# Attention and mixture of experts in one kernel: routing steps placed inside the attention loop

## What is computed

```python
h = _layernorm(x, axis=-1) * (1 + ca) + sa
x = x + ga * _L0_attn_ref(h, ...)        # 16 heads of 16 channels, softmax over 1024 keys
h = _layernorm(x, axis=-1) * (1 + cb) + sb
x = x + gb * _L0_ffn_ref(h, ...)
...
scores = sigmoid(xf @ gate_weight.T)     # 32 experts in 8 groups
sfc = scores + e_score_correction_bias   # best 4 groups by maximum, then best 6 experts
tw = scores of the 6, divided by their sum, times 2.5
routed = sum over the 6 experts of tw * (silu(g) * u) @ down.T
shared_out = (silu(xf @ shared_gate_w.T) * (xf @ shared_up_w.T)) @ shared_down_w.T
return routed + shared_out
```

## Time and profile before

| | us |
|---|---|
| runs | 1714.81, 1718.88, 1721.71 (median 1718.88) |
| the profiled execution | 1716.23 |
| its span, first to last instruction | 1714.5 |
| VectorE busy in the span | 1267.9 (74%) |
| TensorE busy (products) | 1355.5 (79%) |
| ScalarE busy | 795.5 (46%) |
| GpSimd busy | 432.8 (25%) |
| mean granted TensorE clock | 0.885 of full speed |

### The profile page before, as it was taken

One profiled execution on the slowest core, in us unless ns is written; L12 is line 12 of the kernel. 1 busy time (PEld: TensorE's weight loads), 2 busy tenths in 40 slices (PEclk: granted clock), 3 DMA queues, 4 the chain that ended last, 5 costly groups with the idle time before them and its releaser, 6 DMA issues. The chain is left out here.

```text
span 1714.5 us, 33047 instructions
## 1 busy us (share of the span) xinstructions
PE 1355.5 (79%) x8063; PEld 693.4 (40%) x8064; DVE 1267.9 (74%) x3027; ACT 795.5 (46%) x1195; POOL 432.8 (25%) x454
## 2 busy tenths in 40 slices
PE   7963999999998999999937666671299999999800
PEld 4530222233332333322215444441177777777700
DVE  7865999999997999999225677774056555555579
ACT  4650177777776777777812211220033333333300
POOL 0000000000000000000010677777455555555500
PEclk9985599999999999999977878785599999999955
DMA  7857833232222222200064456435765555555497
GB/s 249 257 190 111 178 86 73 66 79 66 63 66 45 68 69 74 65 15 15 20 154 105 153 169 196 152 111 195 264 177 171 166 168 168 169 173 167 132 377 315
DMA packets 221129, 237.34 MB, mean 138 GB/s; under 512 B 96797, under 2 KB 188317, under 8 KB 220898
## 3 DMA queue, kind: packets, MB, share of 16 engines
q1 hardware_dynamic: 191426, 162.23, 35.8%
q0 software_dynamic: 20096, 62.83, 9.6%
q10 hardware_dynamic: 9504, 11.01, 1.8%
HBM read 130.83 MB, written 105.14 MB: 138 GB/s over the span
## 5 line engine op out<-in xcount | busy, mean ns | idle before, releaser
L568 DVE TENSOR_REDUCE piece_max<-psM 128x1 f32<-128x512 f32 x1024 | 634.5, 681 | 34.5 <-PE psM L641 30.6
L623 ACT ACTIVATE probs<-psE 128x1024 f32<-128x1024 f32 x512 | 498.2, 1021 | 227.9 <-PE psE L651 226.4
L641 PE MATMUL psM<-k_main,q_main 48*128 48x512 bf16 x1024 | 319.3, 403 | 59.5 <-DMA v_cols<-v_values 40.9
L663 PE MATMUL psO<-probs,v_cols 128*32 128x512 f32 x2048 | 274.8, 609 | 0.6 <-ACT probs L623 0.6
L1330 POOL DMA_INDIRECT results<-ex_y,ex_pair x223 | 213.7, 958 | 187.6 <-DVE ex_y L1314 122.8
L651 PE MATMUL psE<-q_main,k_main 49*128 49x512 bf16 x1024 | 246.7, 382 | 5.9 <-issue 3.5
L651 PE MATMUL psE<-q_rest,k_rest 48*128 48x512 bf16 x1024 | 246.1, 381 | 0.0
L1242 PE MATMUL ex_psGU<-gu_w,ex_xT 128*128 x892 | 233.2, 384 | 0.7 <-ACT ex_xT L1274 0.5
L641 PEld LDWEIGHTS psM<-k_main,q_main 48*128 48x128 bf16 x1024 | 74.4, 93 | 384.7 <-DVE piece_max L568 308.9
L707 POOL DMA_INDIRECT lists<-rows,slot x192 | 193.0, 1005 | 58.7 <-issue 58.7
L824 POOL MEMSET ones<- 128x128 bf16 x1 | 0.2, 205 | 754.2 <-POOLq L424 754.2
(11 more groups left out here) (167 smaller groups left out, 1363.5 us busy)
## 6 DMA issues: line engine op xcount, KB each, us to landing
ex_rows<-lists SPq DMA_DIRECT2D x223, 160.0 KB, 2.8
six<-results SPq DMA_DIRECT2D x16, 1536.0 KB, 10.0
qk_parts<-parts SPq DMA_DIRECT2D x32, 384.0 KB, 2.6
xin<-in_x_dram SPq DMA_DIRECT2D x16, 512.0 KB, 5.0
v_values<-vst SPq DMA_DIRECT2D x32, 256.0 KB, 3.5
v_cols<-v_values SPq DMA_DIRECT2D x16, 512.0 KB, 4.5
gu_w<-in_guT_dram SPq DMA_DIRECT2D x8, 1024.0 KB
q_main<-qk_parts SPq DMA_DIRECT2D x96, 64.0 KB, 2.9
```

The lines of the kernel that those rows point to most:

```text
L568: nc.vector.tensor_reduce(piece_max[:, (x * PAIRS + h) * KT + qt, kh:kh + 1], psM[:, n % RING], AX.X, ALU.max).then_inc(piece_read, 1)
L623: nc.scalar.activation(probs[:, s % 2, 2 * pair:2 * pair + 2], psE[:, pair], ACT.Exp, scale=HD ** -0.5).then_inc(exp_ok, 1)
L641: nc.tensor.matmul(psM[:, n % RING], qa[g][rows, h, qt * P:(qt + 1) * P], ka[g][rows, h, kh * 512:(kh + 1) * 512], start=True, stop=True). ...
L663: mm = nc.tensor.matmul(psO[32 * h:32 * h + 32], va[g][:, kt, 32 * h:32 * h + 32], probs[:, s % 2, 2 * pair + x], start=(kt == 0), stop=(k ...
```

## The change

All of routing but the last chunk moves into the attention loop, where `route_phase` had it behind. Chunk c (its heads are groups 2c and 2c+1) is routed in window c, the 32 steps that begin with step 32(c+1). `w` is the step in the window, and `d = 4w + n` the place beside the n-th piece of that step, at which VectorE does one part of `route_part`. TensorE's products for routing (two halves of the projection, two halves of the turn, gate, placement) go into the `psM` slot of the next step's first piece, at w = 9, 10, 20, 21, 22, 28. ScalarE copies the turned tile out and takes the sigmoid. GpSimd adds the bias to `x`, normalises and modulates, and scatters.

The softmax sums are now stored as 16 equal rows per head, loaded spread (`inv`, 1024 per partition), and inverted and multiplied there by VectorE (d = 24, 25); `den`, `invert` and its DMAs are gone. The standard deviation's inverse comes from an integer first guess and three rounds of Newton on VectorE (19 small instructions with mean and variance) in place of ScalarE's square root. The experts are picked by `max` and `match_replace` in place of `max_index` and one-hot tiles. The turned tiles of chunks 0 to 5 are kept in DRAM (`h2T_d`).

Behind attention, without a barrier between, `closing_phase` routes chunk 7 and computes the shared expert of all eight chunks, in the order 6, 0 to 5, 7. SP, no longer ScalarE, writes the pads, and the table goes out behind them. The first row load of the experts waits for `y_read`, the last shared expert. Weights of the experts are loaded over the q and k tiles in attention's last batch. The batches are written out, with no loop.

Helpers and parts (TensorE, ScalarE, VectorE):

```diff
+def slot_of(step):
+
+    return 4 * ((step + 1 + AHEAD) % STEPS) % RING
...
+def project_half(pe, env, c, half, to):
+
+    if half == 0:
+        pe.wait_ge(env.vals_ok, c + 1)
+        pe.wait_ge(env.wo_ok, c // CPB + 1)
+    out = to.rearrange("p (i d) -> p i d", i=TPC // 2)
+    for i in range(TPC // 2):
+        at = (half * TPC // 2 + i) * P
+        for m in range(KC):
+            mm = env.nc.tensor.matmul(out[:, i], env.vals[:, m, at:at + P], env.wo_g[:, m], start=(m == 0),
+                                      stop=(m == KC - 1))
+    mm.then_inc(env.projected, 1)
...
+def turn_half(pe, env, c, k, to):
+
+    if k == 0:
+        pe.wait_ge(env.h2_ok, c + 1)
+    for i in range(TPC):
+        mm = env.nc.tensor.transpose(to[:, i * P:(i + 1) * P], env.rows_of(c)[:, i, k * P:(k + 1) * P], env.ident[:])
+    mm.then_inc(env.turned, 1)
...
+def gate(pe, env, c, to):
+
+    pe.wait_ge(env.h2T_ok, KC * (c + 1))
+    for i in range(TPC):
+        for k in range(KC):
+            mm = env.nc.tensor.matmul(to[:, i * E:(i + 1) * E], env.h2T_of(c)[:, k, i * P:(i + 1) * P], env.gate_w[:, k],
+                                      start=(k == 0), stop=(k == KC - 1))
+    mm.then_inc(env.gated, 1)
...
+def place(pe, env, c, to):
+
+    pe.wait_ge(env.sel_ok, c + 1)
...
+def turned_out(act, env, c, k, of):
+
+    act.wait_ge(env.turned, KC * c + k + 1)
+    if k == 0:
+        wait(act, env.h2T_out, 16 * min(c, LAST - 1))
+    env.nc.scalar.activation(env.h2T_of(c)[:, k], of, ACT.Copy).then_inc(env.h2T_ok, 1)
...
+def scores_of(act, env, c):
+
+    act.wait_ge(env.logits_read, c + 1)
+    wait(act, env.routed, c)
+    env.nc.scalar.activation(env.sc[:].rearrange("p i e -> p (i e)"), env.logits[:], ACT.Sigmoid).then_inc(env.sc_ok, 1)
...
+    if d == 24:
+        dve.wait_ge(env.vals_in, 16 * VALS_LOADS * (c + 1))
+        then(v.reciprocal(env.inv[:].rearrange("p k n -> p (k n)"), env.inv[:].rearrange("p k n -> p (k n)")))
+    elif d == 25:
+        ready()
+        v.tensor_tensor(env.vals[:], env.vals[:], env.inv[:], ALU.mult).then_inc(env.vals_ok, 1)
+    elif d in (40, 44):
+        half = (d - 40) // 4
+        dve.wait_ge(env.projected, 2 * c + half + 1)
+        dve.wait_ge(env.biased, c + 1)
+        pair = slice(half * TPC // 2, (half + 1) * TPC // 2)
+        v.tensor_tensor(env.x2[:, TPC * c + 2 * half:TPC * c + 2 * half + 2], of.rearrange("p (i d) -> p i d", i=2),
+                        env.xin[:, pair], ALU.add).then_inc(env.x2_ok, 1)
+    elif d == 42:
...
+    elif d == 92:
+        dve.wait_ge(env.gated, c + 1)
+        wait(dve, env.sc_ok, c)
+        v.tensor_copy(env.logits[:], of[:, 0:TPC * E]).then_inc(env.logits_read, 1)
+    elif d == 100:
+        dve.wait_ge(env.sc_ok, c + 1)
+        then(v.tensor_tensor(env.sfc[:], env.sc[:], bc(env.ebias[:].unsqueeze(1), TPC, E), ALU.add))
...
+    elif d == 109:
+        ready()
+        then(strike(env.masked, env.keys, env.unmasked))
...
+    elif d == 116:
+        dve.wait_ge(env.placed, c + 1)
+        wait(dve, env.placed_read, c)
+        then(v.tensor_tensor(env.slot[:], of[:, 0:TPC * E].rearrange("p (i e) -> p i e", i=TPC),
+                             bc(env.following[:, c % 2].unsqueeze(1), TPC, E), ALU.add))
+        v.tensor_tensor(env.following[:, (c + 1) % 2], of[:, TPC * E:(TPC + 1) * E], env.following[:, c % 2], ALU.add
+                        ).then_inc(env.placed_read, 1)
...
+def scale_out(dve, env, b):
+
+    v = env.nc.vector
+    wait(dve, env.projected, 2 * CPB * b)
+    wait(dve, env.biased, CPB * b)
+    ga = env.modb[:, b, 0]
+    v.tensor_tensor(env.wo_g[:], env.wo[:], ga.unsqueeze(1).to_broadcast([P, KC, D]), ALU.mult).then_inc(env.wo_ok, 1)
+    v.tensor_tensor(env.bo_g[:], env.bo_bc[:], ga, ALU.mult).then_inc(env.bo_ok, 1)
```

In `attention_phase` (in this order: helpers, SP, GpSimd, VectorE, TensorE):

```diff
+        def chunk_at(step):
+
+            c, w = divmod(step, WINDOW)
+            return c - 1, w
+
+        def pieces_for(step):
+
+            ahead, share = divmod(step + AHEAD, STEPS)
+            return ahead + 1, 4 * share
...
+            def store(group):
+                b, g = divmod(group, NG)
+                sp.wait_ge(o_read, QH * (group + 1))
...
+                    for to, at in ((env.o_d, 2 * HD * j), (env.s_d, 2 * HD * j + HD)):
+                        sp.dma_start(to[b, g * HG + j].rearrange("r d a -> d r a"), o_sb[at:at + HD]
+                                     ).then_inc(o_stored, 16)
...
+            def load_values(c):
+                b, u = divmod(c, CPB)
+                sp.wait_ge(o_stored, 16 * 2 * HG * 2 * (c + 1))
+                wait(sp, env.projected, 2 * c)
+                wait(sp, env.h2_ok, c)
+                for m in range(KC):
+                    for to, of in ((env.vals, env.o_d), (env.inv, env.s_d)):
+                        sp.dma_start(
+                            to[:, m].rearrange("p (h a) -> p h a", h=H // CPB),
+                            of[b, u * H // CPB:(u + 1) * H // CPB].rearrange("h (m r) d a -> m (r d) h a", m=KC)[m]
+                            ).then_inc(env.vals_in, 16)
...
+            for group in range(NGR):
+                b, g = divmod(group, NG)
+                c = group // 2 - 1
+                if g % 2 and 0 <= c < LAST - 1:
+                    store_turned(c)
+                if group + 1 < NGR:
+                    put_max(group + 1)
+                if g % 2 == 0 and c >= 0:
+                    load_x(c + 1)
+                if b < B - 1:
+                    sp.wait_ge(summed, STEPS * (group + 1))
+                    load(b + 1, g)
+                elif g < NG - 1:
+                    sp.wait_ge(summed, STEPS * (group + 1))
+                    load_gate_up(sp, env, GU_PART * g, GU_PART * (g + 1))
+                store(group)
+                if g % 2:
+                    load_values(group // 2)
 
         @block.gpsimd
...
+            def normalise(c):
+                b = c // CPB
+                pool.wait_ge(env.inverted, c + 1)
+                if c:
+                    pool.wait_ge(env.scattered[(c - 1) % CPB], 16 * TPC * TOPK * ((c - 1) // CPB + 1))
+                for i in range(TPC):
+                    ins = g.tensor_scalar(env.xhat[:, i], env.x2[:, TPC * c + i], env.mean[:, i:i + 1],
+                                          env.rstd[:, i:i + 1], ALU.subtract, ALU.mult)
+                chain.link(ins)
+                chain.link(g.tensor_tensor(env.xhat[:], env.xhat[:],
+                                           env.modb[:, b, 2].unsqueeze(1).to_broadcast([P, TPC, D]), ALU.mult))
+                g.tensor_tensor(env.rows[:, :, 0:D], env.xhat[:],
+                                env.modb[:, b, 1].unsqueeze(1).to_broadcast([P, TPC, D]), ALU.add).then_inc(env.h2_ok, 1)
...
+            add_bias(0)
+            for c in range(LAST):
+                normalise(c)
+                add_bias(c + 1)
+                pool.wait_ge(env.routed, c + 1)
+                scatter_chunk(nc, env, c)
...
+            def beside(step, n):
+                c, w = chunk_at(step)
+                if c >= 0:
+                    if w == 0 and n == 0 and c == 0:
+                        dve.wait_ge(env.consts, CONSTS)
+                    route_part(dve, env, steps, c, 4 * w + n, psM[:, slot_of(step - 1)])
+                if w == 18 and n == 0 and c % CPB and c < LAST:
+                    scale_out(dve, env, (c + 1) // CPB)
...
+            dve.wait_ge(const_in, 16 * 6)
+            for step in range(-AHEAD, ALL):
+                group, first = pieces_for(step)
+                for n in range(4):
+                    beside(step, n)
+                    if group < NGR:
+                        piece_maximum(group, first + n)
+                if group < NGR and first + 4 == PIECES:
+                    finish(group)
...
+            def route_products(step):
+
+                c, w = chunk_at(step)
+                if c < 0 or w not in (PROJECT, PROJECT + 1, TURN, TURN + 1, GATE, PLACE):
+                    return
+                to = psM[:, slot_of(step)]
+                group, n = pieces_for(step + 1)
+                pe.wait_ge(piece_read, min(PIECES * group + n - RING + 1 if n else PIECES * group, PIECES * NGR))
+                if w in (PROJECT, PROJECT + 1):
+                    project_half(pe, env, c, w - PROJECT, to)
+                elif w in (TURN, TURN + 1):
+                    turn_half(pe, env, c, w - TURN, to)
+                elif w == GATE:
+                    gate(pe, env, c, to)
+                elif w == PLACE:
+                    place(pe, env, c, to)
+
+            def slot_free(step):
+
+                c, w = chunk_at(step - 1)
+                if c < 0:
+                    return
+                if w in (PROJECT, PROJECT + 1):
+                    pe.wait_ge(env.x2_ok, 2 * c + w - PROJECT + 1)
+                elif w in (TURN, TURN + 1):
+                    pe.wait_ge(env.h2T_ok, KC * c + w - TURN + 1)
+                elif w == GATE:
+                    pe.wait_ge(env.logits_read, c + 1)
```

(93 more changed lines are left out.)

902 lines of the change are left out of this document (407 added, 495 removed).

## The result

The changed kernel takes 1805.67 us (median of 4 runs, 1802.8 to 1809.32) against 1720.3 for the kernel before, measured beside it: ratio 1.0503, 95% interval 1.047 to 1.0535. It is slower by 85 us. 1722 had been forecast, with a range up to 1765, so the time lies outside the range.

What follows compares the result with a forecast made beforehand. VectorE, busy 601 of 621 us, was taken to bound attention, and a chain over the engines routing. A tail shorter by 240.6 us against terms of +245 gave +4, about 1722 us on the median's scale, range 1680 to 1765.

Steps and rivals of the forecast that it cites:

- Start, +13: Attention's start: VectorE waits for the constants before the first pieces of group 1; 13 us more, bounds 7 and 14.
- Unrolling: Attention loop: straight-line code has no jump back and no half clock after it; 10 us saved.
- VectorE's work: Routing instructions added to VectorE in attention, 19.3 us a chunk; 127 us more, bounds 115 and 145.
- The late load, +63: At w=6, values land ten microseconds late behind SP's next-batch loads: six times 10, 3 for chunk 6; bounds 54 and 87.
- rival D: Values land still later because the previous chunk's scatter falls on SP's loads and stores; 6 us more gives 1758; chance 0.15.
- ScalarE's tables, +8: In attention, the sigmoid's table load and reloading Exp's, 2.84 us in a stretch; 8 us more, bounds 0 and 15.
- GpSimd beside VectorE, +5: At w=18, only scale_out can meet GpSimd's normalise or add_bias: 2.3 us, at most four times; 5 us more.
- Clock behind the load +14: After the wait for values and the reciprocal, TensorE restarts at half clock: 2 us a chunk, 14 together; bounds 0 and 35.
- handover +32: Six routing products each take a psM ring slot, causing idles: 5 us a chunk, 2.5 for chunk 6; bounds 10 and 50.
- B: In attention, small VectorE work and ring reads fill the handovers and table loads: 40 us less, 1682; chance 0.15.
- C: At w=6 the values are in time, so the 63 and 14 us fall away: 1645; chance 0.07.
- E: TensorE becomes attention's bound: slot waits keep it at half clock for seven more steps a chunk, +45: 1767; chance 0.13.

Runs made afterwards that it cites:

- The change of order: Changed kernel with SyncE's queue issuing a finished group's stores and the four value loads ahead of the next batch's 25 loads: 1717.76 us, ratio 0.9986.
- the version with the four edits: Changed kernel with stores and values first, constants awaited at first use, sigmoid from the exponential, scaling at w=12: 1668.34 us; again on another chip 1666.89.

## Why the prediction was wrong

**What bounds, and the tail: right.** The line of the earlier trace rows that says VectorE has nothing to spare held: the waits taken off it in the experiments came out as time. The tail was 128 us where 124 was forecast (112 to 140), and the shared experts end it, as the sum had it, though the pads took 11 us longer than the sum allowed.

**Start, +13: right in kind, measured 17 in the profile.** The constants were issued at 203.1 to 205.6 rather than near 201.7, behind the maxima, and the first pieces came at 212.27 rather than 194.87. Worth 12 to 17.

**Unrolling, VectorE's work and the reciprocal: right.** The loss at the loop jump is gone: of the idle before the reductions only the start's 14.9 us are still put down to "issue"; how much unrolling won no run separates. VectorE's busy time from 202 to the end of attention grew from 602.9 to 741.3 us; less 7 for reductions that lay ahead of 202 before and 8 for the lock below, and with the 8 of the old inverses, its routing work is 131 where 127 was forecast. The reciprocal is 6.55 us for 1024 against 6.2 from a 64-element row; 6.1 by its removal.

**The late load, +63: measured 96. This is the step that failed most.** Its mechanism was the right one, and its place too, but its size was wrong three times. In chunks 0 to 5 I took 10 us from the queue's order. The order alone makes 11.3 (the window without scatters, and the five behind it with them held), 8 us more over the six; the scatters of the chunk before, which the forecast kept for rival D as a cause by itself, add 3 in each of chunks 1 to 5, 16 together. And in chunk 6, "one large weight load stands there instead: 3" was a guess by the number of instructions in the queue. With that transfer ahead and the scatters beside it the issue of the stores was held (6.15 us for one), and the wait was 12.2, 9 more; why an issue is held so long is not shown. The change of order shows what the step as a whole was worth, 88 us.

**ScalarE's tables, +8: measured about 34** (some 10 either way). I counted the two loads against ScalarE's slack and took the rest as hidden behind VectorE's other holds. The loads stop TensorE for 2.4 us, and behind that its clock is at 0.50 for some 10 us, in which VectorE waits for pieces again. The forecast looked for half clock only behind the late values.

**GpSimd beside VectorE, +5: measured about 15** (some 10 either way). The lock lies where it was said to lie, three times and not four; what was missed is again what came behind it: with VectorE held 2.7 us longer, ScalarE stood 4.1 and TensorE 3.2 us.

**Clock behind the load +14, handover +32: 54 left for both.** What is left, 328 less 17 (start), 96, 34, 15, VectorE's work of 129 (127 and 0.35 for each of seven longer reciprocals) and plus the 17 saved by unrolling and old inverses, is 54; it carries the uncertainty of the others, the 17 of unrolling and inverses being the forecast's own. Idles of 11 to 13 us a window, beyond the waits for values, are left in the version with the four edits too, so they don't come from the late load. No run separates handover from clock here; that stays open. One reason given for the clock term was misread: the row at 204 to 206 shows half clock with TensorE counted busy for all 2 us, and from 160 to 192 of that trace too it is counted busy all the time at 0.50, with some 18 products in 10 us. So idling is not what that row shows; with the reciprocal in four, too, the clock fell while TensorE had little work but no long stop.

So the forecast's +245 was short by 33 in the late load, 26 in the tables, 10 in the lock, 4 at the start, and about 10 over the rest, together the 83. All the errors have one sign. The late load's own length was sized too short; in the tables and the lock a stop was priced at its own length or less, and where it also stopped TensorE, what followed cost about as much again.

**The rivals.** B and C, which made the kernel faster, did not come. The change of order makes C's condition nearly true, with 11 us of waits left, and gives 1717.76 where C had 1645: the other terms stood above their forecast too, and the reciprocal still stops the ring. D, a later load through the scatters, came in part: it was to be the whole of a slower result at 6 us a chunk, and was 3. E, half clock through more of a window, came in part as well: 287 us of attention at half clock. The change of order leaves 218 of them and the exponential in place of the sigmoid 229, each alone; the version with the four edits still has 124 to 127. So the late values and the tables were sources of it, and the rest, with the reciprocal and the handing over of slots beside it, is not separated. D and E had been taken as alternatives; parts of both came, and so did a longer wait by the queue's order alone.

## What to carry over

Before work is moved into a loop whose busiest engine has no slack, look for what that engine will wait for, and put the transfers of that input first in their queue: the new order of one queue was worth 88 us. Price a stop not by its own length alone but with what stands still behind it and at what clock that starts again; a stop of 2.4 us of TensorE cost about 5. When two rivals rest on different resources, add them; they don't exclude each other.

## What the runs showed that was not expected

- A single DMA issue on SyncE's queue took 6.15 us, where the median of its line is 0.48, behind one large weight load with scatters beside it; with the scatters held it took 2.99.
- Held scatters (24, some 31 us on GpSimd) added no wait in a window of 110 to 130 us: in the second window they began at 453.58 in place of 421.97, and beside the stores and value loads they had cost 3 to 6.5 us.
- GpSimd's scaling with a scalar per partition takes 1.21 us for 256 elements a partition, 4.84 for the four tiles, about twice what its product or sum of two tiles takes for the same 1024 (2.37 and 2.67):

```profile
497.25 4.84 POOL L844 TENSOR_SCALAR vals_inv<-x,mean,rstd 128x256 f32<-128x256 f32 x4 [45.05 <-DVE rstd L574]
502.17 2.37 POOL L847 TENSOR_TENSOR vals_inv<-vals_inv,modb 128x1024 f32<-128x1024 f32 x1
```
